# Two attention layers and two feed-forward layers on one core: identity matmuls before the first weights arrive, an early ScalarE function table, and the first norms of batches 2 to 7 moved into the attention loop

## The reference

```python
x = x + attention_16_heads(layernorm(x), ctx, ctx)   # Wq, Wk, Wv, Wo with biases
x = x + mixture_of_8_experts(layernorm(x))           # Wg, then W1, relu, W2 of the chosen expert
x = x + attention_1_head(layernorm(x), ctx, ctx)
x = x + ffn_with_rank_one_terms(layernorm(x))        # gelu
# layernorm(x) = (x - mean) / sqrt(var + 1e-5), over the 256 columns
```

## Time and profile before

| | us |
|---|---|
| median of three executions | 401.39 |
| the three | 402.5, 401.39, 400.26 |
| the profiled execution, its own time | 400.18 |
| span of the profile, first to last instruction | 398.4 |
| PE busy | 352.0 (88%) |
| DVE busy | 182.3 (46%) |
| ACT busy | 147.5 (37%) |
| POOL busy | 57.1 (14%) |
| mean granted TensorE clock | 0.97 |

### The profile page before, as it was taken

One profiled execution on the slowest core, in us unless ns is written; L12 is line 12 of the kernel. 1 busy time (PEld: TensorE's weight loads), 2 busy tenths in 40 slices (PEclk: granted clock), 3 DMA queues, 4 the chain that ended last, 5 costly groups with the idle time before them and its releaser, 6 DMA issues.

```text
span 398.4 us, 7836 instructions
## 1 busy us (share of the span) xinstructions
PE 352.0 (88%) x3108; PEld 267.8 (67%) x3108; DVE 182.3 (46%) x533; ACT 147.5 (37%) x333; POOL 57.1 (14%) x95
## 2 busy tenths in 40 slices
PE   3778788898889888877799999999889999997997
PEld 1435465665556564645488989988768889785875
DVE  4853334546556365554255121211299667350410
ACT  0433543554444543523334411211235647332210
POOL 2720000010101000010110000003484321100000
PEclk9999999999999999987679999999999999998999
DMA  8935060603300000000202859991210011021100
GB/s 242 356 74 202 1 212 3 210 15 121 103 2 16 26 2 13 2 13 2 67 0 63 264 175 304 330 287 36 59 48 1 3 49 50 1 63 42 37 20 28
DMA packets 24819, 35.27 MB, mean 89 GB/s; under 512 B 2528, under 2 KB 21344, under 8 KB 24672
## 3 DMA queue, kind: packets, MB, share of 16 engines
q1 hardware_dynamic: 22096, 31.73, 25.0%
q0 software_dynamic: 768, 1.84, 1.6%
q10 hardware_dynamic: 1920, 1.21, 1.1%
HBM read 31.06 MB, written 3.72 MB: 87 GB/s over the span
## 4 chain that ended last, share of the span: by engine, by line
PE 73%; DVE 10%; ACT 9%; issue 3%; DMA 2%; POOL 1%; SPq 0%; DVEq 0%; ACTq 0%; POOLq 0%
PE ps L697 7%; PE ps L556 7%; PE ps L566 7%; ACT heads L806 7%; PE ps L418 7%; PE ps L406 6%; PE ps L675 6%; DVE mneg L1018 6%; PE ps L459 5%; PE ps L438 4%; PE ps L351 4%; PE ps L629 3%; PE ps L503 2%; PE ps L645 2%; DMA xres<-in_x 2%
## 5 line engine op out<-in xcount | busy, mean ns | idle before, releaser
L1018 DVE TENSOR_REDUCE mneg<-ps 112x4 f32<-112x1500 f32 x32 | 55.1, 1720 | 53.4 <-PE ps L406 53.3
L806 ACT ACTIVATE heads<-ps 125x1792 f32<-125x1792 f32 x24 | 40.0, 1666 | 29.8 <-PE ps L423 29.5
L1229 POOL TENSOR_TENSOR rstd<-veps,neghalf 112x1 f32<-112x1 f32 x32 | 18.4, 573 | 208.4 <-DVE veps L985 208.2
L406 PE MATMUL ps<-heads 32*112 32x375 f32 x256 | 28.8, 516 | 15.7 <-ACT heads L806 7.9
L418 PE MATMUL ps<-heads 32*125 32x224 f32 x384 | 29.1, 389 | 11.0 <-DVE mneg L1018 6.4
L351 PE MATMUL ps<-ctxT,w_in 128*128 128x375 f32 x64 | 25.6, 524 | 7.9 <-DMA ctxT<-in_ctxT 6.3
L556 PE MATMUL ps<-xT,ring 128*128 128x112 f32 x256 | 30.0, 275 | 0.3 <-ACT xT L762 0.3
L762 ACT ACTIVATE xT<-ps 128x224 f32<-128x224 f32 x40 | 13.4, 354 | 45.2 <-PE ps L342 45.2
L418 PEld LDWEIGHTS ps<-heads 32*125 32x125 f32 x384 | 16.7, 190 | 19.4 <-issue 15.0
L556 PEld LDWEIGHTS ps<-xT,ring 128*128 128x128 f32 x256 | 29.3, 192 | 0.5 <-ACT xT L762 0.5
L697 PE MATMUL ps<-heads,ring 128*112 128x256 f32 x128 | 29.3, 386 | 0.0
(11 more groups left out here) (139 smaller groups left out, 528.6 us busy)
## 6 DMA issues: line engine op xcount, KB each, us to landing
ring<-in_L_ffn_W SPq DMA_DIRECT2D x16, 1024.0 KB, 6.6
ctxT<-in_ctxT SPq DMA_DIRECT2D x8, 375.0 KB, 11.2
heads<-in_L_ffn_W SPq DMA_DIRECT2D x2, 1024.0 KB, 9.4
ring<-x_by_odd_rows_dram SPq DMA_DIRECT2D x4, 448.0 KB, 3.6
ring<-in_mask SPq DMA_DIRECT2D x1, 1312.5 KB, 7.0
expert_in_dram<-eo SPq DMA_DIRECT2D x1, 896.0 KB, 10.6
b2row<-in_L_ffn_b SPq DMA_DIRECT2D x8, 112.0 KB, 7.8
xn<-expert_in_dram SPq DMA_DIRECT2D x2, 448.0 KB, 4.8
```

Of the source, the lines that this page charges most:

```text
L406: mm = pe.matmul(bank(j)[0:S, 0:S2], qz[rows, m, a, b * S:(b + 1) * S], kt[b % 3][rows, m, :], start=True, stop=True)
L806: act.activation(pT[w % 2][0:KC, :, :], ps[0:KC, 0:PAIRS, 0:2 * QW], ACT.Exp, scale=DK ** -0.5)\
L1018: v.tensor_reduce(mneg[:, b % 2, PAIRS * g:PAIRS * (g + 1)], ps[0:S, 0:PAIRS, 0:S2], AX.X, ALU.max, negate=True).then_inc(free, 1)
```

## The change

It has three parts. PE multiplies the identity by itself 18 times (`WARM`) after `consts`, into bank 5, and nobody reads the result. ACT asks for the exponential of one number that nobody reads, after it has issued the bias load and ahead of the issue of Wv. The norms of batches 2 to 7 leave the opening: `FIRST_NORMS` puts those of batches 2 and 3 at the end of pair (-1, 6), of 4 and 5 at the end of (0, 5), of 6 and 7 at the end of (2, 6). Their roots and the addition of bo go to the same pairs on POOL. The counts and the waits follow.

```diff
+WARM = 18
+FIRST_NORMS = {(-1, 6): (2, 3), (0, 5): (4, 5), (2, 6): (6, 7)}
...
-    moments = [(n, b) for n in (1, 2) for b in range(NB)] + [(3, 0)]
-    rows = [(n, b) for n in (1, 2) for b in range(NB)]
+    moments = [(1, 0), (1, 1)]
+    rows = [(1, 0), (1, 1)]
+    for i, u in steps():
+        moments += [(2, b) for stage, b in extras(i, u) if stage == "C3"]
+        rows += [(2, b) for stage, b in extras(i, u) if stage == "L2"]
+        moments += [(1, b) for b in FIRST_NORMS.get((i, u), ())]
+        rows += [(1, b) for b in FIRST_NORMS.get((i, u), ())]
+    moments += [(3, 0)]
...
             def turn_x(c):
-                pe.wait_ge(xn_ready, 2 * (c + 1))
+                pe.wait_ge(xn_ready, ROWS_DONE[1, 2 * c + 1])
...
             pe.wait_ge(consts, 1)
+            for _ in range(WARM):
+                pe.matmul(bank(5)[:, 0:P], ident[:, :], ident[:, :], start=True, stop=True)
             pe.wait_ge(ld["wk"], 16)
...
             act.dma_start(bcol[:, :, :], A["bias_columns"]).then_inc(ld["bias"], 16)
+            act.wait_ge(consts, 1)
+            act.activation(unread[:, :], ident[0:1, 0:1], ACT.Exp)
             act.dma_start(w_in[:, 2, :, :], A["L0_xattn_Wv"].rearrange("(k p) n -> p k n", p=P)).then_inc(ld["wv"], 16)
...
-            for n, group in enumerate((range(0, 2), range(2, NB))):
-                v.wait_ge(ld_x[n], 16)
+            def first_norms(group):
                 for b in group:
                     moments(b)
                 for b in group:
                     normalise(1, b)
...
+            v.wait_ge(ld_x[0], 16)
+            first_norms((0, 1))
...
+            v.wait_ge(ld_x[1], 16)
...
-                    v.wait_ge(xbo_ready, NB)
+                    v.wait_ge(xbo_ready, b + 1)
...
                     if stage in ("ND0", "ND1", "C1", "C3", "L2", "C5", "D5", "C6", "D6"):
                         post(stage, b)
+                first_norms(FIRST_NORMS.get((i, u), ()))
...
-            for b in range(NB):
+            for b in range(2):
                 root(1, b)
...
+            for b in range(2):
+                add_bo(b)
...
+                for b in FIRST_NORMS.get((i, u), ()):
+                    root(1, b)
+                for b in FIRST_NORMS.get((i, u), ()):
+                    add_bo(b)
```

More of the change, by code:

```diff
@@ L194, in build @@
         bq_par = sb("bq_par", [P, DT, 2])
+        unread = sb("unread", [1, 1])
         rden = sb("rden", [S, H])
@@ L505, in post @@
                 elif stage == "C4":
-                    pe.wait_ge(xn_ready, NB + b + 1)
+                    pe.wait_ge(xn_ready, ROWS_DONE[2, b])
                     transpose_x("XT2", b, next_bank(SPARE))
@@ L1005, in _ @@
                     normalise(1, b)
[L1006 to L1012, removed]
+            v.wait_ge(ld_x[0], 16)
+            first_norms((0, 1))
+            v.wait_ge(parity_ready, 1)
+            step(v.tensor_reduce(parity[:, :], blocks[:, :].rearrange("p (j a) -> p a j", a=2), AX.X, ALU.add))
+            v.wait_ge(ld["bias"], 16)
+            v.tensor_tensor(bq_par[:, :, :], bcol[:, 0, :].unsqueeze(2).broadcast_to([P, DT, 2]),
+                            parity[:, :].unsqueeze(1).broadcast_to([P, DT, 2]), ALU.mult)\
+             .then_inc(bq_par_ready, 1)
             v.wait_ge(ones_ready, 8)
+            v.wait_ge(ld_x[1], 16)
             def row_max(b, g):
@@ L1258, in _, with add_bo @@
                    allow_small_or_imprecise_dtypes=True).then_inc(consts, 1)
-            g.wait_ge(xn_ready, NB)
+            def add_bo(b):
+                g.wait_ge(xn_ready, ROWS_DONE[1, b])
+                g.tensor_tensor(xres[:, b, :], xres[:, b, :], browL0[:, :], ALU.add).then_inc(xbo_ready, 1)
             g.wait_ge(ld["rows"], 16)
-            for b in range(NB):
-                g.tensor_tensor(xres[:, b, :], xres[:, b, :], browL0[:, :], ALU.add).then_inc(xbo_ready, 1)
-            g.wait_ge(xbo_ready, NB)
+            for b in range(2):
+                add_bo(b)
             for i, u in steps():
@@ L1275, in _ @@
                             ap=idx_put[:, b:b + 1], axis=0), in_=xn[:, b, :], in_offset=None).then_inc(put, 16)
+                for b in FIRST_NORMS.get((i, u), ()):
+                    root(1, b)
+                for b in FIRST_NORMS.get((i, u), ()):
+                    add_bo(b)
+            g.wait_ge(xbo_ready, NB)
             g.wait_ge(ld["mask"], 16)
```

## The result

The changed kernel takes 404.62 us at the median of 14 runs (402.64 to 409.09), the kernel before 401.38 of 14 (399.66 to 403.11). The ratio is 1.0081, 95% interval 1.0051 to 1.0111: slower by 3.2 us, where 401.9 (399.6 to 404.0) was forecast. The profiled execution took 405.09 us, its span is 403.3, that is 4.9 more than before. All ratios here leave out the slow executions, those more than 1.5% above the quickest of their kernel: the 409.09 is one, the traced execution of e1 (410.52) another, and single ones of the kernel before (471), e11 (591) and e10 (696) are too.

What follows compares the result with a forecast made beforehand. From 16 us to the loop's end, each microsecond a DVE row maximum starts late was taken to cost one. Opening -1.3 and norms +2.3 gave 401.2; 0.7 of the median's spread made it 401.9 us, range 399.6 to 404.0.

Steps and rivals of the forecast that it cites:

- the main mechanism: Attention loop: norms delay DVE's row maxima by 1.56 us at (0, 6), 0.74 at (3, 1), zero at (-1, 6).
- The opening, forecast -1.3: Before the first row maximum: gain of 1.07 at the first values plus 0.3 from the norms, taken as 1.3 us.
- these wait for `wg`, issued at 3.56 and landed 9.4 later, at 12.96: Opening: PE's first values, ready at 12.6, wait for this load and start near 13.05 us.
- the end of the warm-up: Opening: identity matmuls end at 7.45 us, at 8.3 if the clock rises late, 9.9 if it doesn't rise.
- 1.07: Opening: what is left of the 1.5 us gain once the first values wait for `wg`.
- the 0.3 for the norms: Opening: without the norms the first row maximum starts 0.95 behind its scores, at 16.02 instead of 16.32 us.
- "late weights" rival: Opening: weights land 1.5 us late behind the table load, values start at 14.55; 403.3 us, chance 0.06.
- The norms in the loop, forecast +2.3: Three groups of 2.66 us on DVE cost zero at (-1, 6), 1.56 at (0, 5), 0.74 at (2, 6).
- I take zero and keep 0.6: POOL's addition of bo beside DVE's normalisation could cost up to 0.3 us each at (0, 5) and (2, 6).
- the lock: Port pair shared by VectorE and GpSimd: the loser waits, adding up to a POOL addition at each place.
- The clock behind the added waits, a rival with 0.17: Ahead of (1, 0): PE, idle 2.0 us, comes back slow, costing up to 1.7; 403.6 us, chance 0.17.
- I counted 0.5 of the spread as removed by the warm-up: Opening: 0.5 of the 1.2 us between median and profiled run comes from late clock rises and vanishes.

Runs made afterwards that it cites:

- e1: Changed kernel without the 18 identity matmuls and the early table load, so only the norms moved; 1.0081 to the kernel before, 405.23 us.
- e11: e3 with PE's waits for Wo and wg moved from ahead of the first values to the first C3 and C5; 0.9952 to the kernel before, 399.81 us.
- e10: Changed kernel with the norms of batches 4 and 5 at (0, 1), those of 6 and 7 still at (2, 6); 1.0014, 401.86 us.
- e8: Kernel before with only the norms moved, to (-1, 6), (0, 1) and (0, 3), no warm-up or early table load; 0.9973, 401.18 us.
- e12: Kernel before with PE's waits for Wo and wg moved to the first C3 and C5; 1.0003, 401.46 us.
- e14: The changed kernel itself, measured again beside e13; 1.0104 to the kernel before, 404.19 us.
- e5: Changed kernel, but POOL waits until a pair's second batch is normalised before adding bo to either; 1.0043 to the kernel before, 404.12 us.
- e2: Kernel before with the 18 identity matmuls and the early table load, norms left where they were; 0.9985, 401.06 us.
- e4: Changed kernel with POOL's additions of bo moved to (0, 1), (1, 1) and (3, 1); 1.0116 to the kernel before, 406.55 us.
- e13: Changed kernel with unread identity matmuls filling PE's waits, 9 at (0, 6) and 5 at (3, 1); 1.0051 to the kernel before, 403.20 us.
- e9: Changed kernel with the norms of batches 6 and 7 at (0, 3), those of 4 and 5 still at (0, 5); 1.0002, 400.98 us.
- e3: Changed kernel with the norms of batches 4 and 5 at (0, 1) and 6 and 7 at (0, 3), in DVE's gaps; 0.9977, 400.85 us.
- e7: Kernel before with the 18 identity matmuls alone; 0.9990, 401.75 us.
- e6: Kernel before with the early table load alone; 0.9973, 401.99 us.

## Why the prediction was wrong

**The direction and the main mechanism** were right: a row maximum late by the norms ahead of it, at (0, 6) and (3, 1) and not at (-1, 6), and all of it on the chain. The steps that failed:

**The opening, forecast -1.3, measured -0.24 in the trace** (and -0.23 to -0.89 in the nine traces that have all three parts). Two steps and a term failed. The first is "these wait for `wg`, issued at 3.56 and landed 9.4 later, at 12.96": I took one landing as fixed. Issue and landing time added up give 12.96 there, the earliest of the sixteen traces, and 13.1 to 13.8 in the other fifteen, e8 and e12 among them (13.5 and 13.6), whose loads are those of the kernel before. It varies, and no part of the change has a clear share in it: the four kernels without either part have 12.96 to 13.56 (mean 13.32), the ten with both 13.12 to 13.80 (mean 13.58). The second is the end of the warm-up: the sum goes by 7.45, and it ended between 7.42 and 8.88 in the eleven traces with identity matmuls. Each has a trace in which it alone holds the values back, `wg` in e14 and PE itself in e11:

| trace | first key projection starts | `wg` landed | PE idle ahead of the values | first values start |
|---|---|---|---|---|
| e14 | 7.42 | 13.80 | 1.29 | 13.96 |
| changed | 8.46 | 13.75 | 0.26 | 13.98 |
| e5 | 8.31 | 13.12 | none | 13.40 |
| e11 | 8.88 | 13.47 | none | 13.97 |

In the kernel before the values start 1.51 behind the queries (12.61 and 14.12). By that the changed kernel, whose queries start at 12.05, would have had them at 13.56 with `wg` in time: 0.56 gained and not 1.07, and the late `wg` took 0.42 of it. The term is the 0.3 for the norms: the first row maximum starts 1.07 behind its scores in the new trace, not 0.95, so 0.18 is left of it. The "late weights" rival named the right wait with the wrong cause. The times don't decide: e2's interval of -1.8 to +0.6 us holds the forecast as well as nothing.

**The norms in the loop, forecast +2.3, measured +3.16.** The step is "I take zero and keep 0.6" for POOL's addition beside DVE's second normalisation. It costs 0.4 at each place (e5: 1.48 instead of 1.88 at (0, 6)), since both wait for POOL's root, and the addition starts 0.06 ahead of the normalisation in every trace with norms in the loop but e5's. At (3, 1) 0.54 more was lost than forecast: 0.40 is this, 0.07 is D5's first instruction (0.29 instead of 0.22 us, beside POOL's second addition), and the last 0.07 I can't place. The prediction says of the lock that no row isolates it, and bounds the cost by the longest normalisation, 0.3. But the kernel before has the meeting in its own timeline, where POOL adds bo while DVE turns the first row maxima:

```profile
18.53 3.46 POOL L1263 TENSOR_TENSOR xres<-xres,browL 112x256 f32<-112x256 f32 x5
...
20.89 0.46 DVE L1030 CAST mpieces<-mneg 112x8 bf16<-112x8 f32 x1
21.38 0.66 DVE L1031 TENSOR_TENSOR mpieces<-mneg,mpieces 112x8 bf16<-112x8 f32 x1
```

Both take 0.18 and 0.19 us at the median of their 16 places: 0.3 and 0.5 more beside the additions.

**The clock behind the added waits, a rival with 0.17.** The price (1.7) was near the 1.1 to 2.7 us seen; the chance was too low, and I priced it at one place only. It happened in 8 of 12 passes through such a wait, in traces of which e1's and e4's are each the slowest execution of their kernel. The granted clocks of all executions weigh it better. Below 0.969 are 15 of the 23 of the changed kernel (its 14 and e14's 9), and 19 of the 118 of the kernel before in the four sets. On one chip, at equal clock, the changed kernel is 1.8 us above the kernel before (402.70 against a mean of 400.93, at 0.970) or 1.7 (404.14 against 402.40, at 0.965 and 0.966), where all executions together say 4.2. So more than half of the 4.2 goes with the clock, and 1 to 2 us of that with the falls that e13's fillers take away.

**The clock at 24 us, not foreseen.** The changed kernel loses 1.05 there; so do e4, e9, e11, e13 and e14 in about the same size, and e5. These are 7 of the 11 traces with identity matmuls; of the 5 without, none shows it, though PE is idle for 1.80 us at this place in the trace before as in that of the changed kernel, of e2, e3, e4 and e7. The executions point the same way: among the kernels without late norms, 19 of 47 with identity matmuls (e2, e3, e7, e11) have a mean granted clock below 0.969, and 28 of 154 without (the kernel before, e6, e8, e12). It is an unwelcome effect that comes with the warm-up, and in these traces it eats what the opening gains. I have no experiment that separates its cause; it stays open.

**The median.** I counted 0.5 of the spread as removed by the warm-up, because the clock rises late in some executions. That mechanism is real: in e1 and e12, two of the five traces without identity matmuls, it cost the first row maximum 2.2 and 2.0 us, and in none of the eleven with them. But e7's median hardly moves (0.9990). Its own trace loses 0.43 in the opening, where the key projection ends later and still has the table load behind it, and others of its executions lose clock, as above; that the two together eat the gain is argued, not shown.

Put together from the traces: -0.24 for the opening, 3.16 for the late maxima and 1.05 at 24 us make 4.0, and with falls behind the late maxima 5.1 (e14) and more, against 3.2 measured at the first comparison and 4.2 at the second (1.0104). The sum is larger than either for two reasons that the record shows. The trace before is of an execution in which the clock rose early; where it rose late without a warm-up (e1, e12), 2.0 to 2.2 us were lost, and the changed kernel has no such executions in its traces. And a fall at one place can stand for one at another: the trace before has one of its own at 174 us, behind an idle time of 1.96, those of e5 and e9 have none there and get 0.78 us back between (6, 3) and (6, 5). How much each of the two is worth in the medians stays open.

## What to carry to other kernels

Before moving work from an opening into a pipelined loop, read for each candidate place how long the engine idles until its next critical instruction, and put the work only where its whole length, round trips and a neighbour's port included, fits: here 3.0 us in gaps of 1.1 and 1.6 cost 3.2 us, and in gaps of 3.8, 4.2 and 5.7 nothing. An opening that gets faster on its engines can end at its last load, so move the waits for loads to where they are first needed in the same edit (e11, the version that beats both, does both; which of the two wins is not separated). A landing time read from one trace is a sample, and so is the time at which the clock rises. A new wait of 2 us on TensorE can cost more than 2 us, since its clock may fall behind it: compare executions at equal granted clock before a difference is put down to the schedule. And look in the trace before for places where two engines already meet; what they cost each other stood there.

## What the runs showed of the hardware

- TensorE came back from idle times of 1.8 to 2.3 us at 1.2 GHz (granted 0.52 in the window behind in the changed kernel) in some executions, and at 2.4 GHz in others of the same kernel. With 2.0 of the 2.3 us filled with matmuls that nobody reads, it came back at 2.4 GHz in the one trace, and the mean granted clock of the executions was 0.969 against 0.964.
- VectorE and GpSimd held each other up: a product of 8 elements a row took 0.65 instead of 0.17 us and ended with GpSimd's addition, a normalisation took 0.81 instead of 0.41.
- ScalarE's queue issued loads while its table load of 1.28 us ran (table load at 2.33, the next issue at 2.39), so the early table load delayed no issue.
- The granted clock read 1.00 in the first ten microseconds of every trace, whether a record of 375 columns took 0.66 us there or 0.32.
